# Packing a block ahead of the candidate step, and no unused identity products, in the two recurrent units of a graph network

## The reference, cut to what matters

```
def _gru_cell(a, h, W_ih, W_hh, b_ih, b_hh):
    gi = a @ W_ih.T + b_ih
    gh = h @ W_hh.T + b_hh
    i_r, i_z, i_n = jnp.split(gi, 3, axis=1)
    h_r, h_z, h_n = jnp.split(gh, 3, axis=1)
    r = jax.nn.sigmoid(i_r + h_r)
    z = jax.nn.sigmoid(i_z + h_z)
    n = jnp.tanh(i_n + r * h_n)
    return (1.0 - z) * n + z * h
```

## Time and profile before

| what | value |
|---|---|
| median of three runs | 6091.77 us (6090.3 to 6093.33) |
| the profiled execution's own time | 6099.82 us |
| its span, first to last instruction | 6098.0 us |
| PE, DVE, POOL, ACT busy in the span | 61%, 43%, 35%, 18% |
| unit 0, from its first L1427 to its thirteenth | 93.79 us |
| unit 2, the same | 95.50 us |

### The profile page before, as it was taken

The page is one execution under the profiler, slowest core; times in us unless marked ns, Lnnn a source line. Parts: engine busy times, 40 slices in busy tenths (PEclk is TensorE's granted clock), DMA queues, the critical chain, the costliest instruction groups (busy, mean ns, idle before and its releaser), DMA issues. The chain is left out here.

```text
span 6098.0 us, 110296 instructions
## 1 busy us (share of the span) xinstructions
PE 3727.4 (61%) x30524; PEld 2730.8 (45%) x30525; DVE 2634.7 (43%) x7089; ACT 1104.9 (18%) x2166; POOL 2137.2 (35%) x2644
## 2 busy tenths in 40 slices
PE   4453177667776969799898244444454555555556
PEld 3443022222224968798887233333333343434445
DVE  5446676666665533312322233333333333333334
ACT  1221013455673012200011000000000000000002
POOL 4554700000000021111101666665656555555550
PEclk5555598888777989899999555555555555555558
DMA  2000000000113513254443222222222222222220
GB/s 115 0 0 1 2 11 27 33 36 40 49 49 117 182 49 136 100 176 162 174 138 107 47 52 53 53 54 53 57 54 54 57 57 55 60 55 58 55 57 21
DMA packets 173664, 404.77 MB, mean 66 GB/s; under 512 B 47902, under 2 KB 109481, under 8 KB 172809
## 3 DMA queue, kind: packets, MB, share of 16 engines
q1 hardware_dynamic: 52409, 259.35, 12.0%
q10 hardware_dynamic: 69360, 91.59, 5.5%
q0 software_dynamic: 51680, 51.82, 4.9%
HBM read 359.52 MB, written 43.07 MB: 66 GB/s over the span
## 5 line engine op out<-in xcount | busy, mean ns | idle before, releaser
L695 POOL DMA_INDIRECT scr<-ptable,src_i x1566 | 1527.8, 976 | 1044.8 <-POOLq L693 584.4
L664 POOL COPY late<-late 128x256 f32<-128x256 f32 (+1 forms) x65 | 25.2, 388 | 2368.5 <-POOLq L662 2368.5
L965 PE MATMUL ps_g<-arena 128*128 128x192 bf16 x1854 | 410.3, 351 | 501.4 <-issue 489.8
L1032 PE MATMUL ps_zz<-scr,arena 128*128 128x192 bf16 x7203 | 616.0, 248 | 65.6 <-PEq L1030 65.6
L1032 PEld LDWEIGHTS ps_zz<-scr,arena 128*128 128x128 fp8e4 x7203 | 604.6, 99 | 76.1 <-issue 73.4
L899 ACT ACTIVATE arena<-arena 128x384 f32<-128x384 f32 x309 | 161.7, 523 | 2451.1 <-ACTq L898 2003.2
L1635 DVE TENSOR_TENSOR arena<-arena 128x196 int32 x1350 | 480.1, 356 | 5.6 <-issue 5.6
L965 PEld LDWEIGHTS ps_g<-arena 128*128 128x128 bf16 x1854 | 234.6, 139 | 539.9 <-issue 530.6
L1140 PE MATMUL ps_zz<-arena,cand 128*128 128x392 fp8e4 x784 | 239.0, 393 | 333.4 <-PEq L1138 329.9
L1032 PE MATMUL ps_zz<-arena 128*128 128x192 bf16 x4802 | 405.8, 247 | 24.9 <-PEq L1030 24.9
L953 PE MATMUL ps_zz<-sb_w_e,arena 64*128 64x128 f32 x930 | 278.7, 435 | 231.0 <-issue 223.5
(11 more groups left out here) (395 smaller groups left out, 6032.9 us busy)
## 6 DMA issues: line engine op xcount, KB each, us to landing
arena<-a_dram SPq DMA_DIRECT2D x245, 784.0 KB, 4.3
arena<-low_dram ACTq DMA_DIRECT2D x309, 192.0 KB
a_dram<-arena SPq DMA_DIRECT2D x49, 784.0 KB, 3.3
arena<-in_e32g ACTq DMA_DIRECT2D x309, 96.0 KB
scr<-ptable,src_i POOLq DMA_INDIRECT x1566
arena<-in_e16p SPq DMA_DIRECT2D x1, 13387.5 KB, 35.2
x<-in_x_nm SPq DMA_DIRECT2D x1, 1664.0 KB, 8.4
out_nm<-x SPq DMA_DIRECT2D x1, 1664.0 KB
```

The source lines that it names most:

```text
L695: pool.indirect_dma_start(grow[:, g % RING, j, :], None, ptable, bass.IndirectOffsetOnAxis(ap=src_i[:, g * GC + j:g * GC + j + 1], axis=0) ...
L965: last = pe.matmul(ps_d[:, m % 2, 0:3 * H], masks[:, m, :, j], msg_h[:, m, j, :, :], start=j == 0, stop=j == GC - 1)
L1032: last = pe.matmul(ps_z[b % 2][:, 0:3 * H], amat[b][:, i, :], hsp[k % 2][:, i, :], start=(i == 0), stop=(i == NT - 1))
```

## The change

The 16 identity products of each block are left out, and DVE packs block b + 2 ahead of the candidate of block b. Nothing else differs, and the last blocks (`more` false) keep their order.

```diff
                 def block(odd, more=True):
                     gate_products(k, odd)
-                    for i in range(WARM):
-                        pe.matmul(ps_a[:, 0:P], ident_h[:, :], ident_h[:, :], start=True, stop=True)
                     turned()
                     if more:
                         front(True, True)
...
                 def block(b, odd, more=True):
-                    candidates(ps_g_odd if odd else ps_g)
                     if more:
                         stage_free()
                         put(b + 2)
+                    candidates(ps_g_odd if odd else ps_g)
                     mixed(b)
```

## The result

| | before | with the change |
|---|---|---|
| median | 6091.03 us (6089.03 to 6093.33, 4 runs) | 6049.33 us (6041.1 to 6060.36, 4 runs) |
| ratio | | 0.9934, 95% interval 0.9922 to 0.9945 |
| profiled execution, its span | 6099.82, 6098.0 us | 6046.67, 6044.9 us |
| unit 0, first to thirteenth candidate | 93.79 us | 72.54 us |
| unit 2, the same | 95.50 us | 70.92 us |

The change is faster by 0.66%; 6047 us was forecast. Of the 53.1 us by which the profiled spans differ, 45.8 lie in the two units: 21.2 in unit 0 and 24.6 in unit 2. The other 7.3 us lie in stages that the change doesn't touch: unit 0 begins 3.9 us sooner (2151.17 for 2155.09) and the stretch between the units takes 3.4 us less (3740.18 for 3743.61).

A forecast was written before the change was run, and what follows sets the result against it. A chain of waits, no engine full, bounds units 0 and 2. DVE's loop, POOL, ends and clock sum to 71.6 for 93.8 and 72.8 for 95.5 us: 44.9 off the 6091.8 median gives 6047 us, range 6033 to 6062.

The forecast's parts named there:

- The chain and what replaces it: Units 0 and 2: packing leaves the chain of waits; DVE's loop becomes the bound, 5.7 and 6.15 us a block.
- The bare tanh: DVE in unit 0: candidate to mixing, no longer covered by the packing, takes 1.77 us with address work.
- POOL: Unit 0: POOL's instructions falling on DVE's mixing add 0.5 us a block, 5 us in all.
- The bound of 2.0 us a block: Unit 0, at most: each of three mixing instructions waits for one POOL instruction of 0.67 us.
- The ends: Last blocks: eleventh interval 5.1 us, twelfth 3.99 or 4.16; POOL ends unit 0 0.5 us later behind DVE.
- Leaving them out is worth 0 by itself, now and with the new order: The 16 identity products, 1.05 us a block in PE's pause before the turning, cover nothing and nothing waits for them.
- rival 1: PE's clock falls in most pauses: 6063 us with a fall each block, 6079 at half rate throughout; chance 0.14.
- 2 us for unit 2 and none for unit 0: Cost of PE clock falls: three at 0.7 us in unit 2, none in unit 0; pauses 2.2 and 1.8 us.
- The transposes: Skill's objection: the turning doesn't count as busy PE, so falls go on at today's rate, adding 2 to 5 us.
- Rivals 3 and 4: 3: stage_free too late, old chain, 6085 to 6092 us; 4: edge loop refetches code, 6110 us; chance 0.04 each.

The follow-up runs named there:

- no_split: The whole change, with POOL in unit 0 doing only the first of its six instructions on each of the first twelve blocks: 6060.7 us, ratio 0.9926 to the kernel before.
- order_only: The kernel before with only the packing moved ahead of the candidate, the 16 identity products kept: 6056.8 us, ratio 0.9916.
- no_products: The kernel before in its old order, with only the 16 identity products of each block left out: 6145.9 us for 6107.2, ratio 1.0064.
- order_third: order_only run again, on one chip with the change: 5428.6 us for 5474.7 before, ratio 0.991.
- change_again: The unaltered changed kernel run again, on the chip of order_only: 6065.6 us, ratio 0.993 to the kernel before.
- three_ahead: The changed kernel, with DVE packing b + 3 between candidate and mixing and ACT freeing the packed buffer ahead of tanh: 5406.9 us, ratio 0.9881 to the kernel before.
- change_third: The unaltered changed kernel run a third time, on one chip with order_third: 5431.6 us for 5474.7 before, ratio 0.9918.

## Why the prediction was right, and where its steps failed

- **The chain and what replaces it: right.** The packing left the chain, the candidate's waits went from 46.7 to 9.2 us, and DVE's loop became the bound. At full rate that loop took 5.59 us a block in unit 0 without POOL (5.36 and 5.82 in no_split) for a forecast of 5.7, and 6.09 in unit 2 (5.88 and 6.30 in order_only) for 6.15.
- **The bare tanh: right.** Candidate to mixing took 2158.37 - 2156.58 = 1.79 us for 1.77.
- **POOL: right in size, by no_split.** It cost 0.43 to 0.55 us a block for 0.5. The Trainium skill's rule ("SBUF — State Buffer", Who interferes with whom), by which one of the two waits for the other's whole instruction, has a row close to it: L1431, at 2158.37, took 0.89 us beside a POOL instruction that ended at 2158.98, 0.47 more than alone for 0.61 of overlap. The bound of 2.0 us a block was far off: no block's mixing in unit 0 of the change took over 2.46 us, for 1.92 alone.
- **The ends: right.** The eleventh interval was 5.25 and 5.26 us for 5.1, the twelfth 3.95 and 4.16 for 4.0 and 4.2. POOL's last instruction of unit 0 starts 7.78 us behind the thirteenth candidate, for 7.22 before: 0.56 for the 0.5 forecast.
- **"Leaving them out is worth 0 by itself, now and with the new order": wrong for now, roughly right only in sum.** In PE's pause they cost nothing, but they shortened the pause. In the old order they are worth 44 us in the units (no_products). The forecast bounded a fall at 1.7 us, from rows where it came behind the turning; where it comes ahead of it, it is 2.7. A half-rate turning, put at 1.6 us in rival 1 without a row, took 1.73.
- **"2 us for unit 2 and none for unit 0": wrong in place and too small.** Against order_only's 69.3 and 69.8 us, the change's three profiled executions had 3.2, 7.5 and 3.9 us in unit 0 and 1.1, 4.0 and 1.7 in unit 2. The forecast took one mean pause a unit, but the two halves of the loop differ. In the change, pauses between full-rate blocks were 1.26 and 2.55 us in turn in unit 0, for a forecast of 1.8, and 1.76 and 2.2 in unit 2: the longer one of unit 0 is as long as those of before, after which a fall came nine times in 22. POOL lengthens it (halves of 5.38 and 6.67 us in order_third, 5.36 and 5.82 in no_split), but falls came without its work too. Nor does the length of the pause just ahead decide alone, which the forecast took for granted. In unit 2 of the change the turning ran at full rate after 3.10 us and at half rate after 1.76:

```profile
5969.96 0.63 PE L985 MATMUL ps_t<-ident,arena 128*128 128x128 f32 x4 [3.10 <-PEq L982]
...
5982.14 1.08 PE L985 MATMUL ps_t<-ident,arena 128*128 128x128 f32 x4 [1.76 <-PEq L982]
```

What sets the moment of a fall was not found. In the execution of change_again the loss is 11.6 of the 18 us that rival 1 and the forecast priced for a fall in every block, so rival 1 was partly true.
- **The transposes: the Trainium skill's statement ("TensorE: Matmul & The Clock Gate", Part 4: PE-mode transpose) that they don't count as busy the same way isn't borne out here.** Ten fp32 transposes kept the kernel at the time of before, 1.0 (0.9991 to 1.001), where nothing in their place cost 0.6% on the other chip.
- **Rivals 3 and 4: neither.** In the change DVE idled at most 0.41 us ahead of the packing in unit 0, and 0.82 in unit 2, where the loop's end lies in it, so nothing waited at `stage_free` for tanh of the same block; and removing the same 128 matmuls in no_products left the stretch between the units at 3744.2 us for 3743.6.

That 6047 us came so near to 6049 is in part luck. In the units, errors cancel: at full rate the loops of order_only were faster than costed by 0.2 us a block in unit 0 (POOL included) and 0.1 in unit 2, and the clock cost 4.3 us instead of 2. The units then gained 45.8 us for 44.9. Outside them 7.3 us went that no step forecast. And the forecast put the median 8.0 us under the profiled execution, as before, where it lay 2.7 over it: the spans differ by 53.1 us and the medians by 41.7.

## What to carry to other kernels

Work that depends on nothing in a chain, and stands in it only by its place in an engine's program, goes ahead of the wait; then ask what it used to cover (here tanh, 0.8 us a block), and whether it can be moved one step further so that it covers that again. Products that nothing reads may hold TensorE's clock: here they were free to leave out only in the kernel whose pauses were down to 0.5 to 1.7 us (three_ahead). Test the two edits apart, since here one alone loses 0.6% and the other alone gains what both do. Price a half-rate stretch by what it covers: 1.7 us a block where it began behind the turning, 2.7 where it began ahead of it.

## What the runs showed of the hardware that was not expected

- In the old order a pause of PE of 2.5 us was followed by half rate in nine of 22 blocks, one of 3.4 us (no_products) in every block, and the blocks then stayed at 10.2 us. In the new order the turning began at half rate after 1.77 us in change_again and 1.76 in the change, and stayed at full rate after 3.10.
- The edge network, untouched, took 2601 us on one chip (change_again) and 1995 on another (change_third) with the same program, from the first L965 to the last: POOL waited 603 us for free buffers there (L693) and 83 here, with gathers of the same 0.97 us each. What makes it was not tried.
